# First attention's tile boundary: mark planes loaded two tiles ahead, factors before the residual, statistics inside the loop

## The reference, cut to what matters

```
h = maximum(layernorm(x), 0)                       # x: 2048 x 512
x = x + L0(h, adj, rel_pair_index, Wq, bq, Wk, bk)  # first attention: the changed stage
h = maximum(layernorm(x), 0)
x = x + L1(h, adj, W_seq, a1, a2, W_out, b_out)     # second attention: not touched

L0: q = h[sub] @ Wq.T + bq ; k = h[obj] @ Wk.T + bk      # 10000 pairs of the first 1500 rows, 8 heads of 64
    scores[:, sub, obj] = (q * k).sum(-1) / sqrt(64)     # all other entries 0
    scores = where(adj == 0, -inf, scores) ; diagonal = 1e-7
    attn = softmax(scores, axis=2)
    return (attn.sum(axis=0) / 8) @ h
```

## Time and profile before

| what | value |
|---|---|
| median of 3 runs | 1475.72 us (1473.87 to 1476.84) |
| profiled execution, its own time | 1474.6 us |
| its span, first to last instruction | 1473.1 us |
| mean granted clock of PE | 0.898 |
| PE busy / DVE busy / ACT busy | 1175.0 / 976.5 / 798.2 us |
| stage 2: first scores to last tile finished | 180.54 to 788.66 us |

### The profile page before, as it was taken

The page is one execution under the profiler, slowest core; times in us unless marked ns, Lnnn a source line. Parts: engine busy times, 40 slices in busy tenths (PEclk is TensorE's granted clock), DMA queues, the critical chain, the costliest instruction groups (busy, mean ns, idle before and its releaser), DMA issues. The chain is left out here.

```text
span 1473.1 us, 24587 instructions
## 1 busy us (share of the span) xinstructions
PE 1175.0 (80%) x10450; PEld 792.7 (54%) x10450; DVE 976.5 (66%) x1340; ACT 798.2 (54%) x779; POOL 169.1 (11%) x183
## 2 busy tenths in 40 slices
PE   4992055877777777878686994999999999999797
PEld 2440021332222223333343553999999999999743
DVE  4200148888777777883101896889898989988545
ACT  2310144555544555552322446998999889999222
POOL 3477400000000000000000560000000000000001
PEclk9996566988888888988898996999999999999999
DMA  7500200101111111110005751010001100010041
GB/s 264 131 2 1 50 30 7 36 10 38 38 37 38 38 37 35 25 22 15 29 14 142 146 99 62 31 59 31 30 31 55 35 31 31 31 59 2 27 168 71
DMA packets 31544, 75.01 MB, mean 51 GB/s; under 512 B 5425, under 2 KB 10304, under 8 KB 29392
## 3 DMA queue, kind: packets, MB, share of 16 engines
q1 hardware_dynamic: 21296, 49.45, 9.6%
q0 software_dynamic: 10144, 24.05, 9.3%
HBM read 78.76 MB, written 15.61 MB: 64 GB/s over the span
## 5 line engine op out<-in xcount | busy, mean ns | idle before, releaser
L942 ACT ACTIVATE s_masks<-s_s1b,s 128x2048 fp8e4<-128x2048 f32 x208 | 396.7, 1987 | 0.0
L1087 PE MATMUL psum<-s_V,s_masks 128*128 128x198 bf16 x2560 | 352.8, 249 | 15.4 <-DVE s_masks L984 15.4
L1088 PE MATMUL psum<-s_V,nadjT 128*128 128x99 bf16 x2560 | 347.6, 209 | 0.0
L460 PE MATMUL psum<-h,s_WT 128*128 128x512 f32 x512 | 266.0, 647 | 2.4 <-ACT s_WT L508 2.1
L1087 PEld LDWEIGHTS psum<-s_V,s_masks 128*128 128x128 fp8e4 x2560 | 250.2, 98 | 16.0 <-issue 15.6
L1088 PEld LDWEIGHTS psum<-s_V,nadjT 128*128 128x128 fp8e4 x2560 | 250.4, 98 | 0.0
L440 PE MATMUL psum<-f_qk 64*128 64x512 f32 x576 | 162.5, 704 | 109.2 <-PEq L203 61.5
L501 ACT ACTIVATE s_exp<-s_exp,s_negm 128x1536 f32<-128x1536 f32 x96 | 150.7, 1570 | 116.7 <-DVE s_negm L593 116.7
L984 DVE TENSOR_TENSOR s_masks<-s_masks,adjT 128x512 uint32<-128x512 uint32 x256 | 170.2, 686 | 49.4 <-ACT s_masks L942 47.0
L593 DVE CUSTOM_DVE_ANT_0 s_exp<-psum,f_low 128x1536 f32<-128x1536 f32 x96 | 164.7, 1753 | 29.1 <-PE psum L440 29.1
L440 PEld LDWEIGHTS psum<-f_qk 64*128 64x128 f32 x576 | 60.8, 219 | 215.4 <-issue 127.3
(11 more groups left out here) (128 smaller groups left out, 1208.9 us busy)
## 6 DMA issues: line engine op xcount, KB each, us to landing
s_s1b<-s_rows SPq DMA_DIRECT2D x16, 1024.0 KB, 4.6
s_adj<-in_adj POOLq DMA_DIRECT2D x16, 512.0 KB, 5.1
rel_planes<-s_zero POOLq DMA_DIRECT2D x3, 2304.0 KB, 19.1
f_rel<-rel_planes SPq DMA_DIRECT2D x36, 192.0 KB, 2.7
s_x<-x SPq DMA_DIRECT2D x6, 1024.0 KB, 12.3
h<-in_x SPq DMA_DIRECT2D x4, 1024.0 KB, 13.8
f_adj<-in_adj POOLq DMA_DIRECT2D x16, 256.0 KB, 5.2
s_x<-in_x SPq DMA_DIRECT2D x16, 256.0 KB, 3.4
```

Of the source, the lines that this page charges most:

```text
L460: last = pe.matmul(ps[:, 7, :], WT[m % 2][:, b, :], h[:, 2 * m + b, :], start=(m == 0 and b == 0), stop=(m == HA - 1 and b == 1))
L942: act.activation(masks[:, j, :], s1b[b][:, :], ACT.Relu, bias=t["s2"][:, n, 0, j:j + 1], scale=BIG, saturate=False).then_inc(signs, 1)
L1087: pe.matmul(out, masks[:, j, cols], V[:, b, j, :, :], **first)
L1088: last = pe.matmul(out[:, :, DZ:CZ], nadjT[:, j, cols], V[:, b, j, :, DZ:CZ], **then)
```

## The change

SP issues the mark planes two steps earlier than they are used: those of tiles 2 and 3 ahead of its loop, those of tile n+4 at the head of iteration n, which also begins with the store of tile n now and ends with the load of x for tile n+2. On DVE `join_planes` and `factors` stand ahead of `finish`, and `measure` stands in the loop, behind the second pair's `add_head`. On ACT `count(n+1)` stands behind the first head's copy and exponential. No instruction is added or taken away.

```
         @block.sync
         def _(sp):
+            def load_x(n):
+                sp.dma_start(xt[n % 2][:, :], io["x"][n * P:(n + 1) * P, :]).then_inc(x_in[n % 2], 16)
+            for n in range(2):
+                sp.wait_ge(f.marked, n + 1)
+                f.load_related(sp, t, n + 2)
+                load_x(n)
             for n in range(NT):
-                b = n % 2
-                if n + 2 < ET:
-                    sp.wait_ge(f.marked, n + 1)
-                    f.load_related(sp, t, n + 2)
-                if n >= 2:
-                    sp.wait_ge(y_out[b], 16 * (n // 2))
-                    sp.wait_ge(measured, n - 1)
-                sp.dma_start(xt[b][:, :], io["x"][n * P:(n + 1) * P, :]).then_inc(x_in[b], 16)
-                if n:
-                    sp.wait_ge(summed, n)
-                    sp.dma_start(t["x1"][(n - 1) * P:n * P, :], xt[1 - b][:, :]).then_inc(y_out[1 - b], 16)
-            sp.wait_ge(summed, NT)
-            sp.dma_start(t["x1"][(NT - 1) * P:, :], xt[1][:, :]).then_inc(y_out[1], 16)
+                if n + 4 < ET:
+                    sp.wait_ge(f.marked, n + 3)
+                    f.load_related(sp, t, n + 4)
+                sp.wait_ge(summed, n + 1)
+                sp.dma_start(t["x1"][n * P:(n + 1) * P, :], xt[n % 2][:, :]).then_inc(y_out[n % 2], 16)
+                if n + 2 < NT:
+                    sp.wait_ge(measured, n + 1)
+                    sp.wait_ge(y_out[n % 2], 16 * (n // 2 + 1))
+                    load_x(n + 2)
...
@@ ACT, step(n)
                 if 0 <= n < NT:
                     start_w(n)
-                if n + 1 < NT:
-                    count(n + 1)
                 for hd in range(HA):
+                    if hd == 1 and n + 1 < NT:
+                        count(n + 1)
...
@@ DVE, step(n)
-                if n >= 2:
-                    finish(n - 2)
-                    measure(n - 2)
                 if 0 <= n < NT:
                     if n + 2 < ET:
                         f.join_planes(dve, n + 2)
                     factors(n)
+                if n >= 2:
+                    finish(n - 2)
+                if 0 <= n < NT:
                     if n + 2 < NT:
                         f.clear_diagonal(dve, t, n + 2)
...
+                    if p == 1 and n >= 2:
+                        measure(n - 2)
```

## The result

The changed kernel takes 1395.6 us (median of 4 runs, 1395.03 to 1397.28) against 1474.8 before (median of 4), a ratio of 0.9463 with a 95% interval of 0.9447 to 0.948. Forecast were 1397, within 1388 to 1411. The profiled execution took 1395.79 us, its span is 1394.3.

What follows compares the result with a forecast made beforehand. No engine is full: a stage 2 step is a ring, with waits at its boundary. Savings of 49.9 (steps 2 to 9), 0.8 (step 10) and 33.1 (tail) less 5.0 (clock) gave 78.8, so 1397 us, within 1388 to 1411.

Steps and rivals of the forecast that it cites:

- the tail: Stage 2 from step 11's last mask to tile 15 finished: 106.3 us instead of 139.4, 33.1 saved.
- the clock: PE's new 4.9 us gap before the second pair's scores: 0.5 us a step lost, 5.0 in all, bounds 0 and 11.
- Boundary of steps 2 to 9: From a step's last mask to the next loop: 5.87 us instead of 12.75, ACT's last exponentials late, `finish` hidden.
- Planes: At the boundary, mark planes issued a step earlier land over 15 us before use, so DVE no longer waits for them.
- The steps together: Steps 2 to 9: boundary 5.87, loop 27.84, statistics 0.93 make 34.64 us a step; 277.1 in all, 49.9 saved.
- PE never stops: In the tail, with factors ahead of `finish`, `start_w` runs under PE's last products, so PE goes on without a stop.
- The statistics: `measure`, moved into DVE's loop, has nothing to hide it and costs 0.93 us a step, paid in full.
- A+11.5: DVE wants the second pair's scores 11.5 us after loop start: a pair 6.94, two heads 3.6, statistics 0.93.
- No clock loss gives 1392: Whole kernel's forecast time if PE's gap before the second pair's scores cost nothing: 1392 us.
- The count: On ACT behind the first exponential: nothing in steps, at most half a microsecond each; 0.3 three times in the tail.
- PE did not fall behind: Rival: slow scores make the aggregate late and `finish` delays the boundary; 1407 likely, 1411 at worst; chance 0.18.
- The other three: Rivals: tail stays open, 1416, chance 0.07; planes still waited for, 1430, 0.03; PE bound at 1.2 GHz, 1585, 0.02.

Runs made afterwards that it cites:

- e1: Kernel before with only SP's new order, mark planes issued two tiles ahead; 1447.1 us, ratio 0.9804.
- e2: Kernel before with only the factors moved ahead of the residual on DVE; 1464.3 us, ratio 0.9929.
- e6: Changed kernel with the statistics of tile n-3 put into DVE's wait for ACT's exponentials, planes of tile n+5 issued behind tile n's store; 1395.1 us.
- e7: Changed kernel with both the statistics in DVE's wait for the exponentials and nine zero products in PE's gap; 1380.3 us, ratio 0.9363.
- e5: Changed kernel with nine extra zero products on PE before the second pair's scores in steps 1 to 10; 1388.8 us, ratio 0.9411.
- e4: Changed kernel with the count moved back ahead of the first copy on ACT; 1395.5 us, ratio 0.9456.
- e8: Changed kernel with PE's gap filled by its own early turns and the statistics in DVE's wait for the exponentials; 1384.7 us, ratio 0.9385.
- e10: Changed kernel with PE's gap filled by its own early turns, the statistics left in the loop; 1390.7 us, ratio 0.9438.
- e3: Changed kernel with the statistics moved back to the boundary, behind the residual; 1400.2 us, ratio 0.9491.
- e9: Kernel before with the factors ahead of the residual and adjacency rows loaded only once the planes of tile n+2 are in use; 1441.8 us, ratio 0.9778.
- e11: Changed kernel with four extra zero products on PE before the second pair's scores; 1394.4 us, ratio 0.9454.

## Why the prediction was right, and where not

- **The whole.** For the profiled execution 1395.8 was forecast and 1395.79 measured; stage 2 is 79.1 us shorter, forecast 78.8. That it fits to a tenth is luck: steps 2 to 9 took 1.6 us more than the sum has for them, the tail 0.9 less, and the 0.5 each that was allowed for the clock in steps 1 and 10 was not lost (step 1 takes 34.45 us from mask to mask, 34.47 before).
- **Boundary of steps 2 to 9.** Forecast 5.87 us, measured 5.85. As forecast, ACT's exponentials are what is late, by 1.21 us (1.08 forecast), and the residual is hidden before `add_diagonal` with 0.21 to spare (0.1 forecast).
- **Planes.** No wait; e1 shows that this part alone is worth its 32.4 us, less what the clock takes.
- **The steps together.** Steps 2 to 9 take 282.7 us (286.65 to 569.32); the forecast was 277.1 and, of the allowance of 5.0 for the clock, four for these eight steps: 281.1. Step 10 takes 34.68 us, forecast 34.6 without the clock.
- **The tail.** 105.4 us (604.00 to 709.39), forecast 106.3. PE still stops, but for 0.47 us at the head of steps 13 to 15 (1.53 in step 12, 3.11 in step 11), where "PE never stops" was forecast. e2 shows that it is the factors' place that closes the tail up.
- **The clock.** 0.5 us a step was taken between 0 and 1.1; measured were 5.5 us of waits in nine steps, 0.61 each. In all nine steps the scores behind the gap of 4.82 us started at 1.2 GHz (granted clock 0.50 in their first microsecond or so) and took 4.39 to 5.49 us instead of 2.85, but the clock came back at different points, so the gap costs DVE 1.18, 0.62 or nothing. The Trainium skill ("TensorE: Matmul & The Clock Gate", Part 1, What's actually happening) calls the throttled state the default; that the scores met it behind every gap agrees with this. The full charge of 1.1 in each step did not come.
- **The statistics: the step that failed.** "Into the loop, where nothing hides it on DVE ... paid in full" is false as a price. Behind the slow scores they cost nothing: removing them gains 0.5 us at most (e6), but 8.5 us once the scores are fast (e7 less e5; 7.9 of it in steps 2 to 10). The sum came out right all the same, because the prediction measured the scores' lateness from the end of the statistics (its A+11.5 contains their 0.93). So 0.93 and the 0.5 behind it, measured 0.61, together are the later of two things that DVE waits for, and not two prices that can be cashed in singly. The 0.61 had been taken between bounds of 0 and 1.1 without a reason for the middle, so that it came close is luck too. "No clock loss gives 1392" was 3 us too high: e5 has 1388.8. That is the 1.4 by which the forecast as a whole lay above the changed kernel, and 6.8 gained where 5.0 had been set aside.
- **The count.** Taken at nothing in the steps and 0.3 three times in the tail. By e4 its new place costs 1.5 us in steps 2 to 10, through PE's longer gap, which the prediction did not count, and saves 2.8 in the tail. Leaving it where it was would have cost nothing that the times can show.
- **The rivals.** PE did not fall behind: the residual waits for no aggregate in steps 2 to 10. The other three did not happen. The clock came back within the second pair's scores or right behind them in every step.

## What to carry to other kernels

Of two delays that end at the same instruction the shorter is worth nothing by itself, and the longer only what it exceeds the other by: removing one lengthens the wait for the other (e5 6.8 and e6 0.5, together 15.3). So look at what stands right behind a wait before pricing either. When an instruction is moved forward, list the transfers that it releases on other queues: in e2 an earlier W let a load of 256 KB in beside the planes that all waited for. And an engine's idle gap can be worth filling, even with products of zeros, where its next work is on the path (e5).

## What the runs showed of the hardware

- The low clock came behind gaps far shorter than the 9 us of the earlier trace rows: after 2.01 us a set of 12 matmuls took 4.54 instead of 2.85 (clock 0.62 in that window) in four of nine steps of e8, and 4.39 in one of e10. After 0.93 us it never came in steps 2 to 10 of e5 and e7. The gap's length does not settle the loss: behind the same 4.82 us the scores took 5.49, 4.92 or 4.39 in rounds of three steps, and in e3 DVE's waits alternated, about 1.98 and 0.87.
- With a load of 256 KB issued 1.3 us behind them (e2), three loads of 192 KB could be used 7.8 to 8.7 us after the start of the residual in six of eight steps and after 5.6 and 5.7 us in two; where that load is issued later (before, e9) it is 5.3 to 5.8 us in all eight.
- Nine products with a tile of zeros in a gap of 4.82 us, which left 0.93 of it, kept the scores behind it at a granted clock of 1.00 (e5). Four, which left 3.09 us, did not (4.23 to 5.49 us for the scores, e11).
